# An adaptive-layer-norm block of linear attention and experts: one-time work put between the first batches, new engine orders, and 15 extra products into an unread bank

## The reference, cut to what matters

```python
mod = silu(c) @ wmod                      # 16 x 6 x 128: sa, ca, ga, sb, cb, gb
ga, gb = hold(ga), hold(gb)               # sign kept, size at least 0.25
h = layernorm(x) * (1 + ca) + sa
q, k, v = h @ Wq.T + bq, h @ Wk.T + bk, h @ Wv.T + bv
q = softmax(q, 8 features of a head);  k = softmax(k, tokens)
o = layernorm(q @ (k.T @ v, head by head)) * ln_g + ln_b
x = x + ga * (o @ Wo.T + bo)
h = layernorm(x) * (1 + cb) + sb
p = softmax(h @ router_w);  the two largest of 8 are kept
hid = for each chosen expert e: gelu(h @ w_in[e] + b_in[e])
x = x + gb * sum over chosen e: p_e * (hid @ w_out[e] + b_out[e])
```

## Time and profile before

| | us |
|---|---|
| median of 3 runs | 392.83 (391.58 to 394.48) |
| the profiled execution | 392.8 |
| its span, first to last instruction | 391.1 |
| first hidden product, hidden(0,0) | 52.25 |
| first hidden product of batch 1 | 73.83 |

### The profile page before, as it was taken

How to read it: one execution, slowest core, us unless ns; L and a number is a source line. 1 busy time by engine, 2 the same in 40 slices (tenths; PEclk the granted TensorE clock), 3 DMA queues, 4 the chain that set the end, 5 groups by cost and what they waited for, 6 DMA issues and landing times.

```text
span 391.1 us, 8091 instructions
## 1 busy us (share of the span) xinstructions
PE 362.9 (93%) x2502; PEld 327.3 (84%) x2502; DVE 282.5 (72%) x1060; ACT 278.5 (71%) x502; POOL 216.8 (55%) x221
## 2 busy tenths in 40 slices
PE   3657789999999999999999999999999999999995
PEld 3446679889999999899899999898998999988875
DVE  2665586787777888878877778788788787786432
ACT  3333679688787969696887879696969878675740
POOL 2315447373938466483838384664837383754543
PEclk9966579999999999999999999999999999999999
DMA  5570051240706071321606070605224150605061
GB/s 182 151 297 2 0 173 73 80 193 24 247 5 242 29 225 47 157 115 41 231 33 241 3 244 27 240 32 168 106 104 169 38 208 3 217 28 216 32 227 41
DMA packets 18817, 47.83 MB, mean 122 GB/s; under 512 B 2571, under 2 KB 6102, under 8 KB 18518
## 3 DMA queue, kind: packets, MB, share of 16 engines
q1 hardware_dynamic: 18576, 46.90, 33.3%
q10 hardware_dynamic: 198, 0.41, 0.3%
HBM read 42.82 MB, written 4.48 MB: 121 GB/s over the span
## 4 chain that ended last, share of the span: by engine, by line
PE 66%; DVE 9%; issue 6%; DMA 6%; POOL 5%; SPq 4%; ACT 2%; POOLq 0%; DVEq 0%; ACTq 0%
PE pY L684 19%; PE pH L672 6%; PE pH L674 6%; PE pH L673 6%; PE pB L661 4%; PE pQV L641 4%; PE pC L629 4%; PE pC L648 3%; POOL v L355 2%; DVE qn L876 2%; DMA gate_bc<-route_scratch 2%; DMA gates<-gate_scratch 2%; SPq L236 2%; DVE elg_cut L934 2%; PE pA L588 2%
## 5 line engine op out<-in xcount | busy, mean ns | idle before, releaser
L684 PE MATMUL pY<-wout,v 128*128 128x128 f32 x1024 | 128.7, 277 | 1.0 <-DVE v L958 0.7
L684 PEld LDWEIGHTS pY<-wout,v 128*128 128x128 f32 x1024 | 121.7, 193 | 2.2 <-DVE v L958 1.1
L502 ACT ACTIVATE u<-pH,cols 128x512 f32<-128x512 f32 x128 | 86.4, 689 | 49.5 <-PE pH L674 42.8
L344 POOL TENSOR_TENSOR rstd_o<-ve_o,neg_half 128x4 f32<-128x4 f32 x16 | 22.0, 1376 | 104.3 <-DVE ve_o L895 104.3
L958 DVE TENSOR_TENSOR v<-u,gate_bc 128x512 f32<-128x512 f32 x80 | 68.6, 860 | 7.0 <-DMA gate_bc<-route_scratch 3.7
L355 POOL TENSOR_TENSOR v<-u,gate_bc 128x512 f32<-128x512 f32 x48 | 63.7, 1329 | 9.0 <-DMA gate_bc<-route_scratch 9.0
L672 PE MATMUL pH<-h_hi,win_hi 128*128 128x512 f32 x128 | 54.9, 429 | 1.4 <-ACT u L502 1.4
L673 PE MATMUL pH<-h_hi,win_lo 128*128 128x512 f32 x128 | 50.6, 395 | 0.0
L674 PE MATMUL pH<-h_lo,win_hi 128*128 128x512 f32 x128 | 50.5, 394 | 0.0
L349 POOL TENSOR_TENSOR h_lo<-h,h_hi 128x512 fp32r<-128x512 f32 x16 | 22.5, 1405 | 20.2 <-ACT h_hi L440 20.2
L452 ACT ACTIVATE xn<-x_all,nmr,rstd 128x128 f32<-128x128 f32 x64 | 26.2, 482 | 4.5 <-POOL nmr L372 4.5
(11 more groups left out here) (151 smaller groups left out, 781.5 us busy)
## 6 DMA issues: line engine op xcount, KB each, us to landing
gate_bc<-route_scratch SPq DMA_DIRECT2D x64, 512.0 KB, 5.7
x_all<-in_L_attn_x SPq DMA_DIRECT2D x16, 256.0 KB, 6.9
out<-x_all SPq DMA_DIRECT2D x16, 256.0 KB, 2.0
gates<-gate_scratch SPq DMA_DIRECT2D x1, 2048.0 KB, 7.1
gb_bc<-gb_scratch SPq DMA_DIRECT2D x1, 1024.0 KB, 4.6
route_scratch<-gateT SPq DMA_DIRECT2D x64, 4.0 KB
win<-in_L_ffn_w_in SPq DMA_DIRECT2D x1, 512.0 KB, 5.6
wout<-in_L_ffn_w_out SPq DMA_DIRECT2D x1, 512.0 KB, 6.9
```

The source lines that it names most:

```text
L344: pool.tensor_tensor(rstd_o[:, :], ve_o[:, :], neg_half[:, :], ALU.pow).then_inc(s["rstdo_ready"], 1)
L502: act.activation(u[:, e % U, :], pH[:, e % 2, :], ACT.Gelu_apprx_tanh, bias=cols[:, e:e + 1]).then_inc(s["gelu_done"], 1)
L684: i = mm(pY[:, t * P:(t + 1) * P], v[:, e % U, t * P:(t + 1) * P], wout[:, e, :], start=False, stop=(e == NE - 1), skip_group_check=True)
```

## The change

**Functions instead of a head.** The one-time work of each engine is cut into functions that are called between the operations of the first batches. PE: `turn_weights`, `modulation`, `residual_gates`, `gain_centred`; its wait for wo_gain moves to hidden(0, e), and the product goes to the second half of pH. DVE: `columns`, `modulation_columns`, `attention_low`, `centring`, `gained_weight`, `attention_gates`, `expert_gates`, `expert_bias` (which takes in the former state_parts). ACT: `attention_weights`, `expert_high`. POOL: `expert_low`, and `modulation_gates(n)`, which waits at batch 0 for the gates of two batches and at batch 2 for the rest. Other one-time waits become waits of the operation that needs them, `if n == 0`.

**Loads.** Wk and Wo go to ACT's queue, between c and w_mod; Silu waits for c alone; x has four semaphores, so x0 to x3 are issued without a wait; x1, x2, x3 precede the experts' weights; the bias pieces come after the first gates.

```diff
+    FIRST = 2
+    XS = 4
...
+            def load_x(n):
+                w(sp, f"x{n % XS}_loaded", DMA * (n // XS))
+                sp.dma_start(x_all[:, n, :, :], x_v[n]).then_inc(s[f"x{n % XS}_loaded"], DMA)
...
+            load_x(2)
+            load_x(3)
             load_experts()
-            load_x(2)
-            spread_mod_gates()
-            load_x(3)
-            spread_moe_gates()
-            for b in range(-5, NB):
+            store_mod_gates()
+            spread_first_gates()
+            load_expert_bias()
+            spread_later_gates()
+            store_gates(0)
+            spread_gates(0)
+            store_moe_gates()
+            for b in range(-1, 9):
                 step(b)
...
```

```diff
+            def keep_clock():
+                pe.wait_ge(s["siluT_ready"], 1)
+                pe.wait_ge(s["wmod_loaded"], DMA)
+                mm(pH[:, 0, 0:2 * P], ident[:, :], wmod_sb[:, 0:2, :].rearrange("p a c -> p (a c)"), start=True, stop=True)
```

```diff
             def step(b):
+                ek_back(b + 3)
+                hidden(b, 5)
+                combine(b, 0)
+                combine(b, 1)
+                combine(b, 2)
+                hidden(b, 6)
+                gate_turn(b + 1)
+                hidden(b, 7)
+                combine(b, 3)
+                combine(b, 4)
+                hT(b + 4)
+                hidden(b + 1, 0)
+                hidden(b + 1, 1)
+                combine(b, 5)
+                state(b + 3)
+                combine(b, 6)
+                q_turn(b + 3)
+                state_weights(b + 3)
+                combine(b, 7)
+                h2T(b + 2)
+                kT(b + 4)
+                hidden(b + 1, 2)
+                attend_centred(b + 3)
+                hidden(b + 1, 3)
+                moe_bias(b + 1)
+                logits(b + 2)
+                hidden(b + 1, 4)
+                qv(b + 4)
+                attend_project(b + 3)
```

More of the change, by code:

```diff
@@ L403, in _ @@
+            weigh(15, 5)
+            residual2(14)
+            residual2(15)
+            for b in range(16, 26):
                 step(b)
@@ L547, in _ @@
+            gelu(15, 6)
+            gelu(15, 7)
         @block.tensor
@@ new lines, in _ @@
+            q_shift(1)
+            ln2_stats(0)
+            state_out(1)
+            ln2_var(0)
+            q_sum(1)
+            k_inv(1)
+            q_inv(1)
+            q_norm(1)
+            k_max(2)
+            expert_bias()
+            out_var(1)
+            v_bias(2)
+            q_bias(2)
+            route(0)
+            q_max(2)
+            gates_out(0)
+            q_shift(2)
+            residual1(1)
+            gates_turned(0)
+            ln2_stats(1)
+            k_inv(2)
@@ new lines, in _ @@
+            ln2_var(1)
+            q_sum(2)
+            q_inv(2)
+            state_out(2)
+            q_norm(2)
+            weigh(0, 0)
+            k_max(3)
+            out_var(2)
+            route(1)
+            weigh(0, 2)
+            ln1_stats(4)
+            ln1_var(4)
+            gates_out(1)
+            q_bias(3)
+            weigh(0, 4)
+            q_max(3)
+            v_bias(3)
+            q_shift(3)
+            residual1(2)
+            weigh(0, 6)
+            ln2_stats(2)
@@ new lines, in _ @@
+            q_sum(3)
+            k_inv(3)
+            gates_turned(1)
+            q_inv(3)
+            ln2_var(2)
+            state_out(3)
+            weigh(0, 7)
+            q_norm(3)
+            weigh(1, 0)
+            ln1_stats(5)
+            k_max(4)
+            y_gated(0)
+            out_var(3)
+            route(2)
+            q_bias(4)
+            q_max(4)
+            ln1_var(5)
+            q_shift(4)
+            weigh(1, 2)
+            gates_out(2)
+            v_bias(4)
@@ new lines, in _ @@
+            k_inv(5)
+            gates_out(3)
+            weigh(2, 4)
+            q_max(5)
+            q_shift(5)
+            v_bias(5)
+            residual1(4)
+            ln2_stats(4)
+            weigh(2, 6)
+            q_sum(5)
+            ln2_var(4)
+            q_inv(5)
+            gates_turned(3)
+            q_norm(5)
+            weigh(2, 7)
+            state_out(5)
+            ln1_stats(7)
+            k_max(6)
+            y_gated(2)
+            ln1_var(7)
+            weigh(3, 0)
@@ new lines, in _ @@
+            route(4)
+            out_var(5)
+            weigh(3, 2)
+            q_bias(6)
+            gates_out(4)
+            residual1(5)
+            weigh(3, 4)
+            q_max(6)
+            q_shift(6)
+            ln2_stats(5)
+            k_inv(6)
+            ln2_var(5)
+            v_bias(6)
+            q_sum(6)
+            q_inv(6)
+            weigh(3, 6)
+            q_norm(6)
+            weigh(3, 7)
+            state_out(6)
+            y_gated(3)
+            ln1_stats(8)
```

993 lines of the change are left out of this document (760 added, 233 removed).

## The result

| | before | after |
|---|---|---|
| median | 393.54 (391.58 to 394.48, 4 runs) | 402.05 (398.72 to 403.29, 4 runs) |
| ratio to before, 95% interval | | 1.021 [1.0132, 1.0287] |
| profiled execution, its span | 392.8, 391.1 | 398.7, 397.0 |
| hidden(0,0), hidden(1,0) start | 52.25, 73.83 | 44.76, 68.95 |
| mean from hidden(b,0) to hidden(b+1,0), b = 1 to 11 | 21.45 | 23.05 |

The prediction was wrong: 379.0 (371 to 388), faster, was forecast; the changed kernel is slower by 2.1%, with an interval from 1.3% to 2.9%. hidden(0,0) came 7.5 us earlier, nearly as forecast. The middle lost it: from hidden(b,0) to the next the times are 24.19 (b = 0), 22.85, 23.25, 26.76, 25.31, 22.35, 22.00, 23.29, 22.22, 21.96, 22.72, 20.86, where before they were 21.43 to 21.58.

What follows compares the result with a forecast made beforehand. PE was taken to bound the full batches, one batch's chain the fill. Gains of 9.2 (fill), 3.2 (13 periods) and 1.5 us (tail) sum to 13.9, span 391.1 to 377.2; forecast time 379, range 371 to 388.

Steps and rivals of the forecast that it cites:

- Edits costed at nothing: the x loads with four semaphores and no wait among the first four: Start of the fill: new x load issue costs nothing; a late x1 would hold modulation_columns 0 to 1 us.
- Rival 1: ACT becomes the bound: one exposed table load a batch gives 397; whole gain gone over period 22.2; chance 0.07.
- slower: Whole kernel: the chance given to the change making it slower, 0.07.
- the drain: ACT table switches: about 1380 ns beside each load by the Trainium skill, 4 us a batch, 435; chance 0.01.
- Fill: Start to hidden(0,0): one-time work no longer ahead of batch 0, so hidden(0,0) at 44.5 instead of 52.25.
- Between hidden(0,0) and hidden(1,0): First full stretch: 18.5 us of work plus 3.3 of holes, hidden(1,0) at 66.3 instead of 73.83.
- The period: One full batch in the middle: 21.2 us instead of 21.45, over 13 periods a gain of 3.2 us.
- ACT: Full batch: four table loads instead of two make ACT 19.7 us busy of 21.2, nothing exposed.
- The sum: Whole kernel: gains 9.2 + 3.2 + 1.5 = 13.9 us, span 391.1 to 377.2, forecast 379.
- rival 3: Whole kernel: only the fill gains, period and tail stay as before, 384; chance 0.14.
- The tail: Last batches: only three combines behind hidden(15,7) instead of six, gain 1.5 us, bounds 0 to 3.
- Rival 2: Fill: the keep_clock products don't hold the clock, some 8 us of path work takes twice as long, 387; chance 0.12.

Runs made afterwards that it cites:

- loads_back: x_early with Wk and Wo back on SP's queue and modulation_columns ahead of ln1_stats(1): 383.81, ratio 0.9777.
- x_early: The changed kernel with each x load issued one batch earlier on SP, nothing else: 384.68, ratio 0.9803.

## Why the prediction was wrong, step by step

- **The step that failed: "Edits costed at nothing: the x loads with four semaphores and no wait among the first four".** It looked at the first four loads only. The lead of the loads in the middle step was never priced, though the diff shows load_x(b+5) in SP's step b, and DVE's step b ends with ln1_stats(b+5). The earlier trace rows and the page of before had what was needed: a spread of 2 MB took up to 7.2 us, and the x load stands behind one. Priced: 7.6 us to landing against no lead, up to some 7 us of DVE idle in a batch where its slack doesn't cover it. It cost 17.4 us (402.05 to 384.68), more than the forecast gain of 13.9.
- **Rival 1 had the right sign and the wrong engine.** It had the whole gain eaten when the period is over 22.2, and the middle took 23.05 on average, but by DVE behind SP's queue; ACT wasn't the bound, and with x in time and without any table load the period is 21.54. That the sign agrees is luck. Its 0.07 for "slower" also leaves out the 0.01 of the drain.
- **Fill, right in its end.** hidden(0,0) was forecast at 44.5 and came at 44.76. It was reached by errors that cancel in part, so its nearness is in part luck: kT(0) at 15.59 in place of 13.2, behind three late transfers, the rows of constants and w_mod, which stand behind Wk and Wo (1.40 and 0.84 us of PE waits), and x1, taken at nothing with a bound of 1 us, for which DVE stood 1.66 us ahead of `modulation_columns` (loads_back gives 13.92); qv(1) at 28.23 in place of 26.9; the round from there to hidden(0,0) took 16.5 us where 17.6 was summed. The gates came in time, as forecast: the second piece was issued at 25.05 and gated_weight(2) ran at 37.30 without waiting for it.
- **Between hidden(0,0) and hidden(1,0), mis-sized.** 3.3 us of holes were forecast; gate_turn(0) alone waited 2.53 (forecast 0.9), moe_bias(0) 1.01, and behind these waits the clock was 0.50 from 51.6 to 55.0, which the forecast didn't have. hidden(1,0) came at 68.95 against 66.3, so 2.6 us are missing here.
- **The period, mis-sized.** 21.2 was forecast and 21.64 measured with the x loads in time: 9 x 0.44 = 3.9 us. The prediction costed DVE by the durations of the old order's rows, and those of operations with their operands in SBUF hold only where POOL rests. With two of POOL's passes shortened the period is 21.18. One of the prediction's own rows was such a row: the 0.98 us that it took for q_norm began 0.03 us behind a pass of POOL (25.61, 0.45 us), while the same operation has a mean of 701 ns over the 16 batches of that trace.
- **ACT, right.** 19.7 us a batch were forecast; x_early has 175.75 / 9 = 19.5. All four loads of a batch together cost 0.1 us there.
- **The sum, mended.** x_early's span is 383.0, 5.8 over the forecast 377.2. The two terms above, hidden(1,0) late by 2.5 (68.76 there) and 3.9 in the middle, make 6.4. The two periods between them, 21.88 and 23.24, are 2.7 over 2 x 21.2, and what follows hidden(12,0) takes 74.4 where the forecast leaves 77.7, which is 3.3 less: 5.8 in all. The 23.24 is work moved forward, 169 records of PE against 158 in the period before it, and the end has the less to do; the prediction spread its gain evenly over 13 periods. So rival 3, with 384, has x_early's number but not the reason: its fill gained less than that rival says, and its nine middle periods are longer than before (21.64 against 21.45). The tail's 1.5 us wasn't tested by itself.
- **Rival 2, the clock.** With the products it stood at 1.00 in most of the fill. Without them the medians are 1.2 and 1.7 us higher, not the 8 that doubling PE's path work would give; in one of the two traces the clock mostly stood without them, in the other it fell and hidden(0,0) came 2.2 us later.

## What to carry to other kernels

When an order is changed, list for each load the step in which it is issued, what stands before it in its queue and the first operation that wants it, and compare the lead with the landing time on the page: a load issued in the step of its use behind a 2 MB broadcast cost more here than all the reordering gained. Durations of small VectorE operations belong to an order, not to the operation: look at what GpSimd runs beside them before they are carried over to a new one. An added delay may cost a lot where taking the same kind of delay away gains next to nothing, so test a suspected bound in both directions.

## What the runs showed that was not expected

- **A VectorE operation with its operands in SBUF can be held for the length of GpSimd's pass.** In the fill of x_early a subtraction of 128 columns began 0.01 us after a pass of POOL and ended 0.15 us after it, while the same subtraction took 0.29 us in the kernel before:

```profile
39.06 2.50 DVE L1336 TENSOR_TENSOR bout_part<-bout_ld,bout_hi 128x128 f32<-128x128 f32 x1
41.59 0.28 DVE L1338 TENSOR_SCALAR bout_part<-bout_part,low_row 128x128 f32<-128x128 f32 x1
```
```profile
39.05 2.36 POOL L356 TENSOR_TENSOR win_lo<-win,win_hi 128x1024 fp32r<-128x1024 f32 x1
```

  DVE's sum with an operand in a bank of PSUM (v_sb, 679 ns before and 679 ns in x_early) and its reductions (qmax, 686 and 685 ns) didn't grow; a TENSOR_SCALAR of four columns (ve, L1358) grew from 171 to 641 ns in the mean of the nine middle steps. The Trainium skill (SBUF — State Buffer, Who interferes with whom) states this as a rule: VectorE and GpSimd share one pair of ports, an exclusive lock that the first to start holds for its whole instruction, and VectorE wants it for two inputs in SBUF or for a copy, cast or tensor_scalar in a mode with two ports, and never for a reduction. These rows agree with it. The prediction didn't use it, and it speaks against what mis-sized the period: carrying DVE's durations over from the old order.
- **An extra pair of table loads costs 0.4 us in one order and 1.9 in the other, while taking all of them away gains 0.2 and 0.1 a batch.** The price of a load isn't linear. Since the pairs stand at different places, one of them chosen for its idle time, these runs don't compare the orders; they show that the first loads were nearly free in either and that one more in the new order was not.
- **A lost lead costs 17.4 us in one order and 133 in the other** (402.05 against 384.68; 525.29 against the 392.4 of before), the latter with a mean clock of 0.87.
